# Four-layer transformer kernel: the later blocks of batch 1 run in halves of 256 tokens, with the work of VectorE, ScalarE and GpSimd beside them in a new order

## The reference

```
0  causal softmax attention, 16 heads of 128, with rope, biases and an inner layernorm and residual
1  out = (gelu(x Wg) * (x Wu)) Wd         2048 hidden units, weights from 4-bit codes and scales
2  q, k, v = split(x Wqkv); q, k = elu + 1 of them
   out = q * cumsum(k * v) / (q * cumsum(k) + 1e-9), all elementwise along 512 tokens; out @ Wout
3  out = (silu(x Wg) * (x Wu)) Wd         688 hidden units, each weight one of 16 table entries
```

## Time and profile before

| what | us |
|---|---|
| median of 3 runs | 672.77 (671.9 to 673.45) |
| the profiled execution, its own time | 671.11 |
| span of its trace | 669.2 |
| busy in the span: PE | 551.3 |
| busy: DVE | 515.9 |
| busy: ACT | 432.9 |
| busy: POOL | 389.1 |
| mean granted TensorE clock, share of full | 0.948 |

### The profile page before, as it was taken

The page is one execution under the profiler, slowest core; times in us unless marked ns, Lnnn a source line. Parts: engine busy times, 40 slices in busy tenths (PEclk is TensorE's granted clock), DMA queues, the critical chain, the costliest instruction groups (busy, mean ns, idle before and its releaser), DMA issues. The chain is left out here.

```text
span 669.2 us, 10939 instructions
## 1 busy us (share of the span) xinstructions
PE 551.3 (82%) x3848; PEld 334.4 (50%) x3848; DVE 515.9 (77%) x1058; ACT 432.9 (65%) x925; POOL 389.1 (58%) x317
## 2 busy tenths in 40 slices
PE   6678988879799999989878988879965997684493
PEld 2346655556466666655654545435532654343252
DVE  7599999979789998998789886746469493586653
ACT  4589888877776688779866675367543486551242
POOL 2798998999988777877736765201441151164021
PEclk9799999999999999999999999969979998995697
DMA  7144653533433565442352230210001000000000
GB/s 260 64 106 113 137 112 103 134 85 75 56 68 76 81 173 86 68 78 59 73 129 81 80 95 0 64 31 13 1 23 41 26 6 2 0 1 0 0 32 31
DMA packets 98389, 44.58 MB, mean 67 GB/s; under 512 B 88224, under 2 KB 90656, under 8 KB 98336
## 3 DMA queue, kind: packets, MB, share of 16 engines
q1 hardware_dynamic: 97344, 43.35, 28.5%
q10 hardware_dynamic: 992, 0.55, 0.3%
HBM read 21.86 MB, written 1.05 MB: 34 GB/s over the span
## 5 line engine op out<-in xcount | busy, mean ns | idle before, releaser
L492 POOL TENSOR_TENSOR qkl<-turned,qkh 128x512 f16<-128x512 f32 (+1 forms) x44 | 60.9, 1384 | 169.2 <-ACT qkh L731 169.2
L1336 PE MATMUL bank<-xTh,w_all_h 128*128 128x512 f16 (+1 forms) x304 | 118.5, 390 | 11.6 <-DVE w_all_l L939 6.6
L1336 PE MATMUL bank<-xTl,w_all_h 128*128 128x512 f16 (+1 forms) x304 | 118.3, 389 | 0.0
L1336 PE MATMUL bank<-xTh,w_all_l 128*128 128x512 f16 (+1 forms) x304 | 118.0, 388 | 0.0
L622 ACT ACTIVATE bank<-bank,nmax 128x128 f32<-128x128 f32 (+3 forms) x128 | 64.0, 500 | 42.6 <-DVE nmax L983 42.1
L462 POOL TENSOR_TENSOR rr<-turned 64x512 f32<-64x512 f32 x64 | 82.2, 1285 | 15.2 <-DVE turned L994 10.2
L470 POOL TENSOR_TENSOR qkl<-rr,qkh 128x512 f16<-128x512 f32 x64 | 73.8, 1157 | 28.7 <-ACT qkh L641 26.2
L463 POOL TENSOR_TENSOR rr<-turned 64x512 f32<-64x512 f32 x64 | 81.3, 1271 | 3.7
L1168 DVE SCALAR_TENSOR_TENSOR turned<-bank,turned 128x512 f32<-128x512 f32 (+1 forms) x44 | 30.1, 683 | 60.9 <-PE bank L1336 32.2
L731 ACT ACTIVATE qkh<-turned 128x512 f16<-128x512 f32 (+1 forms) x44 | 27.6, 627 | 65.4 <-DVE turned L1168 65.4
L1005 DVE SCALAR_TENSOR_TENSOR parts<-bank,rscaled,parts 128x128 f16<-128x128 f32 (+3 forms) x128 | 65.4, 546 | 0.4 <-ACT parts L633 0.3
(11 more groups left out here) (190 smaller groups left out, 1557.9 us busy)
## 6 DMA issues: line engine op xcount, KB each, us to landing
stage<-in_per_head SPq DMA_DIRECT2D x16, 512.0 KB, 4.2
xa<-in_codes SPq DMA_DIRECT2D x32, 128.0 KB, 2.7
stage<-in_packed SPq DMA_DIRECT2D x12, 256.0 KB, 3.1
stage<-in_scales SPq DMA_DIRECT2D x12, 256.0 KB, 3.6
pT<-parts SPq DMA_TRANSPOSE x128, 2.8
x<-in_x SPq DMA_DIRECT2D x2, 512.0 KB, 7.0
stage<-in_w1T SPq DMA_DIRECT2D x2, 512.0 KB, 3.7
out<-x SPq DMA_DIRECT2D x2, 512.0 KB, 2.9
```

Source lines behind the costliest of these rows:

```text
L492: pool.tensor_tensor(il[n % 2][0:rows, :], inter[0:rows, n % 2, :], ih[n % 2][0:rows, :], ALU.subtract).then_inc(g_il, 1)
L1336: last = pe.matmul(dst, l, r, start=start and i == 0, stop=stop and i == 2, skip_group_check=skip)
```

## The change

1. Batch 1 is cut in two units of 256 tokens from run 2 on. A step of run 2 now takes one unit and two hidden tiles: 8 steps for unit 2 (tokens 0 to 255 of batch 1), then 8 for unit 3. Run 4 does the same with 3 and 3 steps. `pieces_of` says which tiles, columns and row tiles belong to step n. Run 1 and run 3 (batch 0) keep 512 tokens a step.
2. The layernorms of batch 1 after blocks 1, 2 and 3 are made for two row tiles at a time (`ROWS_OF`), and those of batch 0 for four as before.
3. The reciprocal of the standard deviation is made by POOL (`rstd_of`: add the epsilon, then raise to the power -0.5) and no more by ACT and DVE.
4. Block 2 runs in four units of 256 tokens, each with both feature halves side by side in one bank of 512 columns. `1 + elu` is made as min(exp, 1) + relu in one DVE instruction (`feature`); the running sums carry over from one unit to the next, and an `ones` row with a zero in its middle splits the scan. POOL makes numerator and denominator product.
5. Comparisons come for 2 x 512 columns in one instruction (8 instead of 16 a piece), have two sets of target arrays, and start in run 1, after step 12. The look-ups start in run 1, step 14, and the order of pieces is `HIT_AT`, `LOOKED_UP_AT`, `CODES_AT`.
6. The orders of all four engines beside the steps are written anew.

The core of the diff:

```diff
+HIT_AT = {12: 0, 13: 1, 14: 2, 15: 3, 16: 4, 18: 5, 20: 6, 25: 7, 28: 8}
+LOOKED_UP_AT = {14: 0, 15: 1, 16: 2, 17: 3, 18: 4, 19: 5, 24: 6, 31: 7, 32: 8}
+UNIT = S // 2
+ROWS_OF = ((0, TPB), (TPB, 2 * TPB), (TPB, TPB + 2), (TPB + 2, 2 * TPB))
...
+        def pieces_of(n):
+            if RUN2 <= n < RUN3:
+                unit, j = B + (n - RUN2) // RUN2_HALF, (n - RUN2) % RUN2_HALF
+            elif n >= RUN4:
+                unit, j = B + (n - RUN4) // RUN4_HALF, (n - RUN4) % RUN4_HALF
+            else:
+                return (n - (n >= RUN3) * RUN3,), slice(0, S), range(TPB)
+            return (2 * j, 2 * j + 1), tokens(unit), range(2 * unit, 2 * unit + 2)
...
+            def rstd_of(phase, part, what):
+                n, rows = event(phase, part, what), row_slice(part)
+                scale = 1.0 if what == "x" or (phase, part) in COPIED else ATT1_SCALE if phase == 2 else FFN_SCALE
+                pool.wait_ge(d_var, n + 1)
+                pool.tensor_scalar(var_eps[:, rows], mv[:, rows, 1], LN_EPS / scale ** 2, None, ALU.add).then_inc(g_var, 1)
+                pool.wait_ge(g_var, n + 1)
+                pool.tensor_tensor(rstd[:, rows], var_eps[:, rows], minus_half[:, rows], ALU.pow).then_inc(g_rstd, 1)
...
-            def std_of(event, eps=eps_ln):
-                act.wait_ge(d_var, event + 1)
-                act.activation(std[:, :], mv[:, :, 1], ACT.Sqrt, bias=eps[:, 0:1]).then_inc(a_std, 1)
...
+            def entries_hit(pair):
...
+                for e in range(LUT // 2):
+                    if pair >= 2 and e % 4 == 0:
+                        dve.wait_ge(t_lut, 2 * (pair - 2) + e // 4 + 1)
+                    last = dve.tensor_scalar(hot[pair % 2][e][:, :, 0:n], idx16[pair % 2][:, :, 0:n], entry[:, e:e + 1], None, ALU.is_equal)
...
+            def feature(u, w):
+                dve.scalar_tensor_tensor(out=phi[u % 2][:, w, :], in0=expo[:, w, :], scalar=1.0, in1=pos[:, w, :],
+                                         op0=ALU.min, op1=ALU.add).then_inc(d_phi, 1)
...
+            def look_up(pair, part):
+                pe.wait_ge(d_hot, 2 * pair + part + 1)
+                if part == 0:
+                    pe.wait_ge(a_lut, LUT // 2)
+                    if pair:
+                        pe.wait_ge(a_w2, 2 * pair)
+                n = CHUNKS[pair][1]
+                for e in range(4 * part, 4 * part + 4):
+                    for i in range(2):
+                        last = pe.matmul(side_bank[1 - i][:, 0:n], spread[:, e, :], hot[pair % 2][e][:, i, 0:n],
+                                         start=e == 0, stop=e == LUT // 2 - 1)
...
+            for m in range(I_TILES):
+                if m == RUN4_HALF:
+                    turn_half(3, 3)
+                    turned_half(3, 3)
+                gate_up(RUN4 + m, table_weights(1), i_rows, beside_fourth, 2 * m)
```

More of the change, by code:

```diff
@@ L1542, in down, with gate_up @@
-            def down(n, m, before, weights, rows):
-                r = rows(m)
-                if m == 0:
-                    if before in BY_ACT and before not in COPIED:
-                        pe.wait_ge(a_y, BY_ACT.index(before) + 1)
-                    else:
-                        pe.wait_ge(d_acc, SUMS.index(before) + 1)
-                    open_sums()
-                pe.wait_ge(g_il, n + 1)
-                ws = weights(2, m, 0)
-                for t in range(TPB):
-                    hs = [a[n % 2][0:r, t * P:(t + 1) * P] for a in (ih, il)]
-                    last = product(row_tile(t), hs, ws, False, False, skip=True)
+            def gate_up(n, weights, rows, beside, k):
+                tiles, columns, _ = pieces_of(n)
+                width = S // len(tiles)
+                for w, (banks, done) in enumerate(((G_bank, t_gate), (U_bank, t_up))):
+                    if n >= 2:
+                        pe.wait_ge((a_gelu, d_inter)[w], n - 1)
+                    for i, m in enumerate(tiles):
+                        for c in range(KC):
+                            last = product(banks[n % 2][0:rows(m), i * width:(i + 1) * width], weights(w, m, c),
+                                           x_parts(columns, c), c == 0, c == KC - 1)
+                    last.then_inc(done, 1)
+                    beside(k + w)
@@ new lines, in down @@
+            def down(n, weights, rows):
+                tiles, _, row_tiles = pieces_of(n)
+                width = S // len(tiles)
+                pe.wait_ge(g_il, n + 1)
+                for i, m in enumerate(tiles):
+                    ws = weights(2, m, 0)
+                    for j, t in enumerate(row_tiles):
+                        o = i * width + j * P
+                        hs = [a[n % 2][0:rows(m), o:o + P] for a in (ih, il)]
+                        last = product(acc_bank[t // 2 % 2][:, t % 2 * D:t % 2 * D + D], hs, ws, False, False, skip=True)
@@ L1641 @@
+            down(RUN4 + I_TILES - 1, table_weights(1), i_rows)
 def kernel(**inputs):
```

998 lines of the change are left out of this document (560 added, 438 removed).

## The result

The changed kernel takes 648.07 us (median of 4 runs, 646.8 to 651.28), the kernel before 672.74 beside it (671.9 to 673.45). The ratio is 0.9641, with a 95% interval of 0.9604 to 0.9679: faster by 3.6%. The forecast was 638.1 with a range of 625 to 656. The profiled execution took 647.89, with a span of 646.1.

What follows compares the result with a forecast made beforehand. No engine is full; PE waits for chains through the others. Work 171.6, idle 30.1, clock 5 and contention 3 make 209.7, so PE ends at 628.4, span 634.5, median 638.1 us; range 625 to 656.

Steps and rivals of the forecast that it cites:

- work: PE from 418.7 us to its last matmul: matmuls counted at full clock, 171.6 us.
- clock: PE slowed behind waits of 3 to 4 us: 5 us lost, between 0 and 10.
- contention: POOL's low halves slowed while DVE compares: 3 us, between 0 and 19; as a rival 19, giving 654, chance 0.14.
- Halves on PE: Runs 2 and 4 and projections: 12 matmuls of 256 columns cost 1.3 as 6 of 512 did, so nothing.
- Place 4: End of run 3: late low halves of step 4 and of x for unit 2 of run 4; PE waits 5.5.
- place 5: Run 4 before step 3: statistics, passes, norms, turn and halves outlast 5.3 of PE work beside; PE waits 3.4.
- place 6: Run 4, steps 3 to 5: norms of batch 0 and unit 2 stand before products on DVE; PE waits 3.8.
- the wait of step 8: Run 2, step 8: piece 6 needs `weighted` of unit 1, behind reciprocal, `attend` and two features; PE waits 1.7.
- place 3: Run 2, steps 10 to 12: low half 3.9 late, project1 of unit 2 3.7, two small waits; 8.6 in all.
- Place 1: Look-ups, run 1 step 15 to run 2 step 4: waits at pieces 1 to 4 and the turn, 7.1 in all.
- The POOL pass: 19 passes of two small operations on POOL replace square roots on ACT: 0.6 us each with inner wait.
- The rival of the slow pass: 14 of 19 POOL passes on PE's path: gain used up from 3.1 a pass, 677 at 3.4; chance 0.04.

Runs made afterwards that it cites:

- run 2: Not a follow-up run: a stretch of the kernel's own gate_up and down steps, for batch 1, cut by the change into 8 steps for each of two units; no time of its own.
- run 4 whole: Changed kernel with run 4 alone back to whole steps of 512 tokens and one column tile, its norms and turn in front: 655.42 us, ratio 0.9746.
- The first experiment: Changed kernel with xTl of the second turn made ahead of the comparisons of step 13 of run 1, not behind them: 647.36 us, ratio 0.9606.
- Doubling: Changed kernel with the sum and the power of each inverse-deviation pass on POOL done twice, with waits between, same result: 668.42 us, ratio 0.9938.
- the experiment: Changed kernel with each comparison of 1024 columns back to two of 512, 16 a piece instead of 8: 652.61 us, ratio 0.9735.

## Why the prediction was right, and where it was off

- **Direction, size, range: right.** 24.7 us came out where 34.7 were forecast. From 418.7 to the last matmul I had 209.7; it is 220.8 (639.55 - 418.7). The 11.1 between them are some 6.2 of work, 4.6 of idle time and 3.4 of clock, less the 3 for contention that didn't come: three terms were too low, and the one that was too high hid a part of it.
- **Halves on PE: the spacing was right.** Matmuls of 256 columns start 0.11 apart with a load of 0.10 between them, also in the long series of run 4 (610.00, 610.11, 610.22). By the rule of the Trainium skill that I had weighed against this ("TensorE: Matmul & The Clock Gate", section Back-to-back issue gap), short matmuls pay for their loads; at 256 columns no run here shows it. "Nothing" is a little too low all the same: with run 4 whole the work is 1.2 less (table), for 72 matmuls.
- **Idle: 30.1 forecast, some 35 measured, at the places named.** Place 4 had 5.5 and has 6.4 (2.87 + 3.49), place 5 had 3.4 and has 4.65, place 6 had 3.8 and has 4.9, the wait of step 8 had 1.7 and has 1.61, place 3 had 8.6 and has 6.7. Place 1 had 7.1 and has 9.3, in another form (pieces counted from 0): piece 4 has 3.11 (3.7), and piece 1 has 0.51 where I put 1.9, but piece 0, to which I gave no wait, has 4.76. The step that failed was "its comparisons and xTl delay the product before": I let them delay a product and not the first look-up itself, which waits for that `xTl`. The first experiment showed that this miss costs under 1 us in the end. (Of the waits before, "the largest" leaves out two of 5.5 and 4.9, at 495.74 and 517.10; the sum of 52.0 has them. The terms listed for place 5 add up to 8.3 and not 8.7, so to 3.0.)
- **The POOL pass: mis-sized, by a wrong argument.** I took 0.6, "what the old route cost without table loads". That figure is right for the old route (0.58 in front of run 4); the pass measured this, by its groups (ns, minimum, median and maximum):

```profile
L556 POOL TENSOR_SCALAR var_eps<-mv x19: 219/231/664, 241.8 to 640.7; 128x2 f32<-128x2 f32 x10, 128x4 f32<-128x4 f32 x9
L558 POOL TENSOR_TENSOR rstd<-var_eps,minus_half x19: 713/1036/1452, 242.1 to 641.0; 128x2 f32<-128x2 f32 x10, 128x4 f32<-128x4 f32 x9
```

  From the variances to the result a pass is 1.1 for two tiles and 1.5 for four, and 2.0 where a low half stands before it on POOL, as at 632.07 (0.97 of it is that wait). The power takes 0.71 for 2 columns and 1.04 for 4, 0.17 a column; "the small rows go with size", my argument against the slow pass, came from a sum whose columns cost next to nothing. The 0.5 and 0.9 by which I missed ten and nine passes are 13.1 us of POOL. Doubling added 22.9 of POOL and 12.2 of PE's idle time; by that slope, an estimate, the miss is worth some 7 of idle time, and clock behind it. Of the idle time 4.6 more than forecast came out, so that I counted other waits some 2 too high, as at place 3. The rival of the slow pass had its mechanism right: at 2.3 to 2.7 a pass the gain is all but used up (ratio 0.9938), where I had put the point at 3.1; it came sooner, in part since that sum leaves out the slow clock that the longer waits bring.
- **ACT's table loads: counted as a benefit that the old order never paid.** I wrote "17 x 1.28 = 22 us less of ACT", which is true of ACT's busy time. The pass alone in the old order makes the kernel 0.6% slower; the roots put back in the new order cost 8.7. So the pass needs the order; the rest of the change with the old roots still gains 2.2% (ratio 0.9776).
- **Comparisons: right.** 1024 columns start 0.40 apart as forecast, and the experiment puts their worth at 4.5 to 5. One in each of several pieces takes 1.37 instead of 0.47 while POOL has a low half (row of DVE's timeline of the changed kernel):

```profile
418.84 1.37 DVE L1236 TENSOR_SCALAR ol<-xT,entry 128x1024 f16<-128x1024 f16 x1
```

- **Contention: 3 forecast, nothing on POOL.** No low half is above 1.47 now, where one was 4.55 and another 3.42 (534.57). With comparisons of 512 columns in the new order the longest is 1.47 too, and in the pass alone, with the old order and the old comparisons, 2.07. So neither their length nor the old order by itself makes the 4.55; what did is open.
- **Clock: 5 forecast, 8.4 measured, 7.7 of it in the four stretches above; about 5 were paid.** What I hadn't seen is that a slow stretch is free where it lies in front of a wait for a longer chain.
- **The end: 6.1 forecast, 6.6 measured**, the difference again the pass: 1.14 of wait where I had 0.5.
- **Work: the largest miss.** The prediction has 171.6 for PE's work; 177.8 were measured. Of the 6.2, 1.2 is that run 1 began 1.16 later in this execution, so that more of it was left at 418.7; 1.6 is that the count was low for the kernel before already (173.2 by the table, at 418.7); and 3.4 came with the change (174.4 to 177.8), of which run 4's halves explain 1.2. The rest I didn't separate.
- **What wasn't tried**: the halves of run 2 by themselves, since its norms, turns and projections would all have to be put in another order. Undone one at a time, the pass, the wide comparisons and the halves of run 4 are worth 8.7, 4.5 and 7.35; these need not add up, and how much of the 24.7 the order and the halves of runs 2 and 3 bring by themselves isn't shown.

## What to carry to other kernels

A wait before a low half or a copy was seldom the price of the work itself here: look on the engine that makes it for what stands in front, and put the piece that TensorE waits for ahead of norms and comparisons that nobody waits for yet; this was worth 18 us (648.07 to 630.19), beside 24.7 for the change. By the table 11.9 of it were waits and 6.7 the clock behind them, so take idle time and slow clock apart before a run is called for or against a theory of a wait. Price an operation that is moved to another engine by the time its reader waits for it in either place, not by the busy time that it takes off the first. A time that TensorE loses at the lower clock or in one wait counts only if no wait for a longer chain follows.
